# An attention stage on one NeuronCore: the small products of a sequence stand beside the four groups of value products

## What is computed

```python
x = x + recurrence(layernorm(x))
z = layernorm(x)
h = layernorm(z) * g1 + b1
q, k, v = h @ Wq, h @ Wk, h @ Wv            # 16 heads of 8
attn = softmax(q @ k.T / sqrt(8))           # 256 x 256 a head and sequence
z = z + (attn @ v) @ Wo
m = layernorm(z) * g2 + b2
wts, idx = top_k(softmax(m @ Wg), 2)        # then the two experts of each token
x = x + z + moe(m, wts, idx)
```

## Time and profile before

| | us |
| --- | --- |
| median of three runs | 1008.87 |
| lowest and highest | 1007.47 and 1013.91 |
| span of the profiled execution | 1007.7 |
| first to last value group of the attention stage | 215.69 to 646.18 |
| PE busy | 768.5 (76%) |
| DVE busy | 794.3 (79%) |
| ACT busy | 635.2 (63%) |
| mean granted clock of PE | 0.900 |

### The profile page before, as it was taken

One profiled execution on the slowest core, in us unless ns is written; L12 is line 12 of the kernel. 1 busy time (PEld: TensorE's weight loads), 2 busy tenths in 40 slices (PEclk: granted clock), 3 DMA queues, 4 the chain that ended last, 5 costly groups with the idle time before them and its releaser, 6 DMA issues.

```text
span 1007.7 us, 25725 instructions
## 1 busy us (share of the span) xinstructions
PE 768.5 (76%) x8206; PEld 464.6 (46%) x8207; DVE 794.3 (79%) x1681; ACT 635.2 (63%) x1278; POOL 525.7 (52%) x665
## 2 busy tenths in 40 slices
PE   3678776689989898989788888849889999993000
PEld 2445454324445443434344444437777888872000
DVE  7789989788888979898988885168888888888512
ACT  6755468647777777777667778328767777772000
POOL 9600379401254725341133778737886066755775
PEclk9989999869999989999889999559999999997555
DMA  8840015312111111111011120114544355543422
GB/s 196 295 151 1 2 63 182 137 34 59 52 47 55 54 44 55 54 34 34 18 33 57 53 64 26 45 36 122 127 120 130 94 125 130 132 119 111 124 73 73
DMA packets 132214, 84.71 MB, mean 84 GB/s; under 512 B 54534, under 2 KB 117642, under 8 KB 132122
## 3 DMA queue, kind: packets, MB, share of 16 engines
q1 hardware_dynamic: 123930, 66.71, 22.9%
q0 software_dynamic: 8192, 16.79, 6.1%
HBM read 30.77 MB, written 41.94 MB: 72 GB/s over the span
## 4 chain that ended last, share of the span: by engine, by line
PE 59%; issue 9%; ACT 9%; POOL 9%; DVE 9%; DMA 1%; ACTq 0%; DVEq 0%; POOLq 0%; SPq 0%
PE bank L1355 55%; ACT arena L857 5%; POOL HT L758 3%; POOL Z L758 3%; PE bank L1542 2%; PE bank L1359 2%; DVE arena L1044 1%; ACT arena L766 1%; PE bank L1549 1%; POOL xh L496 1%; POOL rr L492 1%; DVE arena L1113 1%; DVE mom L963 1%; DVE Z L1028 1%; ACT arena L933 1%
## 5 line engine op out<-in xcount | busy, mean ns | idle before, releaser
L1113 DVE TENSOR_REDUCE arena<-bank 128x2 f32<-128x512 f32 x512 | 329.7, 686 | 45.3 <-PE bank L1355 41.2
L857 ACT ACTIVATE arena<-bank 128x512 f32<-128x512 f32 x512 | 288.1, 596 | 114.1 <-PE bank L1355 112.1
L1355 PE MATMUL bank<-QK 32*128 32x256 f16 (+1 forms) x2048 | 179.0, 284 | 46.1 <-ACT arena L857 28.2
L1355 PE MATMUL bank<-w2p,QK 128*128 x1280 | 205.0, 246 | 1.9 <-DVE arena L1318 1.9
L1355 PE MATMUL bank<-arena,w1h 128*128 128x256 f16 x640 | 162.5, 277 | 8.5 <-DVE arena L1318 5.0
L685 POOL DMA_INDIRECT expert_in<-HT,idx x128 | 132.4, 1034 | 69.1 <-issue 28.8
L933 ACT ACTIVATE arena<-bank,b1s 128x256 f32<-128x256 f32 x320 | 125.4, 474 | 50.5 <-PE bank L1355 44.8
L1355 PE MATMUL bank<-arena,VA 128*32 128x256 f32 x2048 | 145.5, 404 | 0.7 <-ACT arena L857 0.7
L1355 PEld LDWEIGHTS bank<-w2p,QK 128*128 128x128 f16 x1280 | 123.7, 97 | 13.1 <-issue 2.4
L1355 PEld LDWEIGHTS bank<-QK 32*128 32x128 f16 (+1 forms) x2048 | 51.2, 93 | 169.1 <-ACT arena L857 133.0
L1308 DVE TENSOR_TENSOR QK<-arena,QK 128x1024 f16<-128x1024 f32 x80 | 98.0, 1225 | 19.1 <-ACT QK L766 17.1
(11 more groups left out here) (155 smaller groups left out, 1142.4 us busy)
## 6 DMA issues: line engine op xcount, KB each, us to landing
QK<-qk_parts SPq DMA_DIRECT2D x96, 128.0 KB, 2.6
expert_in<-arena SPq DMA_DIRECT2D x40, 256.0 KB, 3.6
expert_out<-arena SPq DMA_DIRECT2D x80, 128.0 KB
qk_parts<-arena SPq DMA_DIRECT2D x16, 512.0 KB, 3.0
X<-x SPq DMA_DIRECT2D x8, 512.0 KB, 5.8
wst<-w SPq DMA_DIRECT2D x16, 256.0 KB, 2.8
out<-arena SPq DMA_DIRECT2D x16, 256.0 KB, 2.4
expert_in<-HT,idx POOLq DMA_INDIRECT x128
```

Of the source, the lines that this page charges most:

```text
L857: nc.scalar.activation(PT[t % 8], bank[3 + t % 2][:, :], ACT.Exp, scale=DH ** -0.5)\
L1113: V.tensor_reduce(nmax[n % 2][:, :, 4 * j + g], bank[u % 3][:, :].rearrange("p (q t) -> p q t", q=2), AX.X, ALU.max, negate=True).then_inc ...
L1355: return nc.tensor.matmul(dst, lhsT, rhs, start=start, stop=stop)
```

## The change

The small products keep their number and form and move on PE. The context's transpose goes from step 5 to step 6, in front of the value group there; the maxima's transpose from step 8 to right behind that group; the normed context's transpose from step 9 to behind the group of step 10; the product with Wo from step 12, and the normed tiles' transposes from step 13, to behind the group of step 14; the bias product's two halves, from steps 0 and 1, the logits' two halves, from steps 3 and 4, and the counts to behind the group of step 2. ACT copies the maxima at step 8 instead of 9 and the normed context at step 11 instead of 10. DVE's reads move with them by one or two steps.

```diff
--- before.py
+++ after.py
@@ -899,9 +899,9 @@
                         exp_gate(0)
                     if b > 0 and c == 3:
                         ctx_evac(b - 1)
-                    if b + 1 < NB and c == 9:
+                    if b + 1 < NB and c == 8:
                         max_evac(b + 1)
-                    if b > 0 and c == 10:
+                    if b > 0 and c == 11:
                         cnt_evac(b - 1)
 
 
@@ -1262,17 +1262,17 @@
                         max_chunk(16 * b + c + LEAD)
                     if stats_at(b) is not None and c < 8:
                         stat5(stats_at(b), c)
-                    if c == 5 and 2 <= b < 2 + NE:
+                    if c == 4 and 2 <= b < 2 + NE:
                         if group_at(b - 7) is not None:
                             dve.wait_ge(lg_done, group_at(b - 7) + 1)
                         b1_add(b - 2)
-                    if c == 6 and group_at(b - 7) is not None:
+                    if c == 4 and group_at(b - 7) is not None:
                         read_logits(group_at(b - 7))
-                    if 16 * ROUTE0 + 6 <= 16 * b + c < 16 * ROUTE0 + 22 or 16 * ROUTE0 + 37 <= 16 * b + c < 16 * NB:
+                    if 16 * ROUTE0 + 6 <= 16 * b + c < 16 * ROUTE0 + 22 or 16 * ROUTE0 + 36 <= 16 * b + c < 16 * NB:
                         next(first_route, None)
-                    if b > 0 and c == 6:
+                    if b > 0 and c == 7:
                         ctx_norm(b - 1)
-                    if b > 0 and c == 13:
+                    if b > 0 and c == 15:
                         ctx_add(b - 1)
             for _ in first_route:
                 pass
@@ -1587,22 +1587,24 @@
                 b, c = t // 16, t % 16
                 if b < NB:
                     scores(t, t + LEAD, True, t + LEAD < 16 * NB)
-                if c % 4 == 2 and 6 <= t < 16 * NB + 6:
-                    pv((t - 6) // 4)
-                if c < 2 and 2 <= b < 2 + NE:
-                    b1_shift(b - 2, c)
-                if c in (3, 4) and group_at(b - 7) is not None:
-                    pe.wait_ge(x3_ready, b - 1)
-                    pe.wait_ge(lg_read, group_at(b - 7))
-                    logits(group_at(b - 7), bank[7][:, 288:288 + 4 * NE], MT, range(2 * c - 6, 2 * c - 4))
-                if c == 3 and b == ROUTE0 + 2:
-                    pe.wait_ge(x3_ready, b - 1)
-                    counts(0, bank[7][:, 320:320 + 2 * NE])
-                if b > 0 and c == 5:
+                if b > 0 and c == 6:
                     if group_at(b - 7) is not None:
                         pe.wait_ge(mt_ready, group_at(b - 7) + 1)
                     ctx_t(b - 1)
-                if b + 1 < NB and c == 8:
+                if c % 4 == 2 and 6 <= t < 16 * NB + 6:
+                    pv((t - 6) // 4)
+                if c == 2:
+                    if 2 <= b < 2 + NE:
+                        b1_shift(b - 2, 0)
+                        b1_shift(b - 2, 1)
+                    if group_at(b - 7) is not None:
+                        pe.wait_ge(x3_ready, b - 1)
+                        pe.wait_ge(lg_read, group_at(b - 7))
+                        logits(group_at(b - 7), bank[7][:, 288:288 + 4 * NE], MT)
+                    if b == ROUTE0 + 2:
+                        pe.wait_ge(x3_ready, b - 1)
+                        counts(0, bank[7][:, 320:320 + 2 * NE])
+                if b + 1 < NB and c == 6:
                     if 2 <= b < 2 + NE:
                         pe.wait_ge(b1_added, b - 1)
                     if group_at(b - 7) is not None:
@@ -1610,12 +1612,13 @@
                     if b == ROUTE0 + 2:
                         pe.wait_ge(cnt_read, 1)
                     max_t(b + 1)
-                if b > 0 and c == 9:
+                if b > 0 and c == 10:
                     ctx_n(b - 1)
-                if b > 0 and c == 12:
-                    ctx_o(b - 1, b + 1 < NB)
-                if c == 13 and group_at(b - 6) is not None:
-                    tp5_group(group_at(b - 6))
+                if c == 14:
+                    if b > 0:
+                        ctx_o(b - 1, b + 1 < NB)
+                    if group_at(b - 6) is not None:
+                        tp5_group(group_at(b - 6))
 
 
             pe.wait_ge(x3_ready, NB)
```

## The result

The changed kernel takes 1120.28 us (median of four runs, 1111.05 to 1124.34), the kernel before, beside it on the same chip, 1008.17 us (1004.54 to 1013.91): 1.1075 times as long, with a 95% interval of 1.102 to 1.1131. The forecast was 1137 with a range of 1068 to 1182, and a chance of 0.90 for slower. The profiled execution has a span of 1109.3 us against 1007.7.

What follows compares the result with a forecast made beforehand. Bound: the score steps' latency loop, where PE waits for ACT's exponentials. Stage 498 at full clock plus 62 for clock falls is 560, 129.5 above 430.5; 1007.7 + 129.5 = 1137 us, range 1068 to 1182.

Steps and rivals of the forecast that it cites:

- The loop: In the score steps, the third step comes 1.07 us behind the pair, because its bank waits for an ACT exponential.
- plain stretches: From one value group's start to the next, four score steps without small products: 2.88 us, before and after the change.
- Prices on PE: Products beside a value group cost, in us: context and normed tiles 0.59, normed context 0.37, maxima and logits 0.54, output 0.64.
- the low end: Products right behind a value group may save 0.15 us each, 17 us less, so 481 us at full clock.
- Prices on ACT: Context's copy 0.59 us a sequence, as now; normed context's copy, moved behind the pair's first exponential, 0.45 new.
- The sum at full clock: Score-step stage with stretches, products, ACT copies and 4 us of routing, before clock falls: 498 us.
- The covers: Maxima's copy, earlier DMA, DVE's moved reads and the maxima transpose's wait for a reduction stay hidden, adding nothing.
- The clock: In the score-step stage, 25 falls to the lower clock (bounds 3 and 50), 2.47 us lost each: 62 us.
- Clock as now: Rival: only three clock falls in the stage, 7 us, giving 1065 to 1082 us; chance 0.22.
- Clock low for half: Rival: the clock stays at its lower level for half of the stage, giving 1184 us; chance 0.13.
- PE is the bound: Rival: PE pays for switching; 180 visits removed at 0.33 us save 59, giving 949 us, faster; chance 0.05.
- The queue covers it: Rival: exponentials that ACT holds when a run begins cover the longer run, giving about 1008 us; chance 0.05.

Runs made afterwards that it cites:

- The first: Changed kernel with the maxima's transpose back at step 8, between pair and third step, and ACT's maxima copy at step 9: 1089.38 us, 1.0812 of the kernel before.
- third: Changed kernel with two useless 32-bit identity products added behind every pair of score steps, overwritten by the next scores: 1086.19 us, 1.079 of the kernel before.
- fourth experiments: Kernel before, with normed context's and normed tiles' transposes, logits and bias halves moved into waits between pair and third step: 988.21 us, 0.9805 of the kernel before.
- The kernel with one run alone: Kernel before, with only the product with Wo and the normed tiles' transposes moved behind the third value group (step 14): 1051.24 us, 1.0401 of the kernel before.

## Why the prediction was right, and where its sizes were off

**The loop.** Right: plain stretches are 2.89, third steps 1.07 to 1.08 behind the pair, and what stands beside a value group adds to the stretch. The first, third and fourth experiments show it from three sides: a product put back is free, useless ones are free, and two in a wait are free.

**Prices on PE.** Right for the normed context's transpose (0.37), the product with Wo (0.64) and the rare run (462.74 to 463.73, 0.99). Too high for two. The maxima's transpose has 16 columns and starts 0.89 behind the value group (450.84 to 451.73), where score steps and the normed context's transpose come after 1.00; with 0.53 to the scores it costs 0.42 and not 0.54. So the saving that I kept for the low end was there, in part, for this product alone. The normed tiles stand behind another full-size product and cost 0.44 instead of 0.59 (458.77, 459.32, 459.85: 1.08 for both, less 0.64). Over the stage these are 4 and 2 us.

**Prices on ACT.** Too high. I took the busy time of a copy, 0.45 and 0.59, where I took the time from start to start on PE. ACT, in order of time, shows the copies of the normed context and of the context:

```profile
456.44 0.47 ACT L875 ACTIVATE arena<-bank,bqkv 128x256 f32<-128x256 f32 x1
456.79 1.68 ACT L857 ACTIVATE arena<-bank 128x512 f32<-128x512 f32 x3
...
464.64 0.59 ACT L766 ACTIVATE arena<-bank 128x512 f32<-128x512 f32 x1
465.12 1.68 ACT L857 ACTIVATE arena<-bank 128x512 f32<-128x512 f32 x3
```

The next exponential starts 0.35 and 0.48 behind them, and the fourth score step is 0.36 and 0.49 late (0.85 and 0.98 behind the third instead of 0.49). That is 3 us each over 31 sequences. The reading of the earlier trace rows was off by another 3 us: the copy of the context alone makes 0.49 into 0.98, so the 1.08 there held 0.10 of the context's transpose, which was not quite free.

**The sum at full clock.** Predicted 498 with 4 for routing, so 494 without; measured 482.7. The four prices above make up these 11 us (4, 2, 3 and 3).

**The covers.** They held. The maxima's transpose shows no wait behind its value group, DVE's moved reads none that matters, and what lies outside the stage kept its length within 2.1 us.

**The clock.** Right in kind, in place and nearly in count: 25 falls were expected, one in each of the 19 bias and logits sequences and 6 in the 12 others; 22 came, 16 in those 19 and 6 in the others. That it is just 6 is luck, since that number was a judgement. Too high in size: I gave each the 2.47 us of a fall of 6.8 us. Most took 3.4 us, such as the one at 259.50, which cost 1.6; five behind logits took 10.2. At the third experiment's 0.38 a us the 126.7 us cost 48 and not 62. These 14 and the 11 of the sum nearly make up the 26 by which the stage, at 534.2, fell short of the 560 of the forecast. The median is nearer to the forecast than the profiled execution is, since that was the shortest of the four; the other three have a lower mean clock (0.864 to 0.866 instead of 0.879; the forecast had 0.84).

The Trainium skill (TensorE: Matmul & The Clock Gate, A second HAM failure mode) has a kernel in which short idles between groups of matmuls are enough to make the clock oscillate. The 22 falls agree, and so does their drop to 9 when the idles were filled.

**The rivals.** *Clock as now* is out: 22 falls against 4. It was also priced too low. The stage before had four falls and 44.8 us at the lower level, which cost 17 us at 0.38 and not the 7 of three falls; that puts this rival at 1075 to 1092. The third experiment, with 51.6 us at the lower level, is nearly this case and came to 1086. In the same way the growth at full clock is 76 us and not 50 to 71: the 430.5 that it was taken from holds 24 us of clock and routing. The forecast is not touched by this, since it counts all falls of the changed stage. *Clock low for half* is out: 126.7 of 534.2 us. *PE is the bound* is out by the sign, and by the useless products that took no time. The Trainium skill (TensorEngine Tiling (Array Packing), Key Properties) has TensorE drained when its tiling mode changes. No row shows a drain as such; that a product of 16 columns starts 0.89 and others 1.00 behind a value group's start would fit a price that goes by shape. The time did not follow it: 180 visits fewer, 11% slower. *The queue covers it* is out: ACT idled for PE 216.0 us.

## What to carry to other kernels

Where an engine waits in a loop of fixed latency, work placed in the wait is free and work placed beside the big groups is not, even if that looks tidier and saves changes of shape; find the wait that recurs and fill it, up to its length. Price a step from the start of an instruction to the start of the next one, on every engine, and follow each semaphore of a moved product to what now stands ahead of its raiser. Idle waits can cost a second time through the clock, which harmless work in them can partly buy back: 34 and 29 us in two kernels here, and nothing that could be told in two others.

## What the runs showed of the hardware that I had not expected

- More work made the kernel faster: 481 more instructions on PE in the stage (5146 against 4665 in the two rows of it), and 34 us less.
- An ACT copy of 0.47 us busy delays what follows by 0.35, one of 0.59 by 0.48.
- A busy PE does not bring the clock back soon in every case. The kernel with one run alone had a fall of 34.1 us, in which PE was busy for 32.21 (the row below, columns as for the stage above). Most falls of the changed kernel took a tenth of that. What sets the length stays open.

```profile
324.70:358.80 34.10, 32.21 (x230) 15.35 (x222) 16.72 (x32) 14.85 (x27) 10.47 (x12) 0.50 0.08 21
```
